# Scatter-adds of a graph diffusion that take turns over three accumulator tables in place of two

## The reference

```
h    = h @ W0.T + b0
deg  = segment_sum(ones, row) over row = [src, loops], col = [dst, loops]
dis  = 1 / sqrt(deg)
agg  = segment_sum(dis[row] * dis[col] * h[col], row)
x    = x + h + 0.05 * (agg - h) + 1.5 * relu(h)
```

## Time and profile before

| | us |
|---|---|
| median of 3 runs | 8765.82 |
| lowest and highest run | 8748.99, 8783.12 |
| span of the profiled execution | 7386.2 |
| what lies between the median and the span | 1379.6 |
| busy in the span: TensorE | 4675.6 (63%) |
| VectorE | 4503.1 (61%) |
| GpSimd | 3795.4 (51%) |
| ScalarE | 1623.3 (22%) |
| HBM read, written | 608.19 MB, 417.84 MB |

### The profile page before, as it was taken

One profiled execution on the slowest core, in us unless ns is written; L12 is line 12 of the kernel. 1 busy time (PEld: TensorE's weight loads), 2 busy tenths in 40 slices (PEclk: granted clock), 3 DMA queues, 4 the chain that ended last, 5 costly groups with the idle time before them and its releaser, 6 DMA issues. The chain is left out here.

```text
span 7386.2 us, 101314 instructions
## 1 busy us (share of the span) xinstructions
PE 4675.6 (63%) x31722; PEld 4192.0 (57%) x31722; DVE 4503.1 (61%) x5720; ACT 1623.3 (22%) x2242; POOL 3795.4 (51%) x3348
## 2 busy tenths in 40 slices
PE   4665335760188785555555866666668774784797
PEld 2354334650177785555555866666568774674675
DVE  6998443222577786666667842232398894683457
ACT  0143112330143343222222421111134340000001
POOL 0198565563277403777771047777600006766766
PEclk9866668995599998766767987777789996997899
DMA  2298666656722374332333753334357883122009
GB/s 75 48 276 259 140 147 140 138 108 201 252 73 73 101 245 154 83 79 79 81 78 101 249 164 109 109 109 112 100 186 250 304 307 112 49 59 91 14 12 278
DMA packets 837873, 1024.59 MB, mean 139 GB/s; under 512 B 589119, under 2 KB 601812, under 8 KB 836380
## 3 DMA queue, kind: packets, MB, share of 16 engines
q1 hardware_dynamic: 534716, 742.63, 31.5%
q0 software_dynamic: 144256, 90.12, 8.3%
q10 hardware_dynamic: 158560, 187.31, 7.6%
HBM read 608.19 MB, written 417.84 MB: 139 GB/s over the span
## 5 line engine op out<-in xcount | busy, mean ns | idle before, releaser
L839 POOL DMA_INDIRECT gc_msgs<-t,src_rows x784 | 754.4, 962 | 1098.1 <-POOLq L146 804.2
L893 POOL DMA_INDIRECT acc<-de_sums,de_put x392 | 608.5, 1552 | 410.9 <-DMA acc<-de_sums,de_put 263.5
L1913 PEld LDWEIGHTS gc_ring<-gc_msgs,gc_hot 128*128 128x128 f32 x4736 | 628.4, 210 | 305.9 <-issue 298.1
L1913 PE MATMUL gc_ring<-gc_msgs,gc_hot 128*128 x4736 | 654.9, 297 | 230.4 <-SPq L1872 229.3
L839 POOL DMA_INDIRECT at2s_ends<-h,src_rows x392 | 369.9, 944 | 533.6 <-POOLq L146 414.4
L839 POOL DMA_INDIRECT at1s_ends<-x,src_rows x392 | 389.2, 993 | 490.5 <-POOLq L146 371.3
L1027 PE MATMUL de_ring<-de_win,de_pick 128*128 x2368 | 343.2, 305 | 272.7 <-DMA de_win<-t 272.7
L1027 PEld LDWEIGHTS de_ring<-de_win,de_pick 128*128 128x128 f32 x2368 | 322.9, 217 | 295.0 <-issue 289.1
L839 POOL DMA_INDIRECT at1s_ends<-x,dst_rows x392 | 419.0, 1069 | 119.5 <-issue 119.5
L839 POOL DMA_INDIRECT re_rows<-x,src_rows x392 | 406.5, 1037 | 125.1 <-issue 124.8
L1393 PE MATMUL re_psR<-w_rel,re_own 128*128 128x128 f32 x3136 | 398.6, 293 | 73.6 <-DVE re_own L1330 73.3
(11 more groups left out here) (471 smaller groups left out, 11359.4 us busy)
## 6 DMA issues: line engine op xcount, KB each, us to landing
rew_win<-x SPq DMA_DIRECT2D x74, 544.0 KB, 4.0
at1w_win<-g SPq DMA_DIRECT2D x74, 544.0 KB, 4.0
at2w_win<-g SPq DMA_DIRECT2D x74, 544.0 KB, 4.0
de_near<-same SPq DMA_DIRECT2D x74, 512.0 KB, 5.1
de_win<-t SPq DMA_DIRECT2D x74, 512.0 KB, 4.6
x<-rew_win SPq DMA_DIRECT2D x74, 512.0 KB, 2.9
h<-at1w_win SPq DMA_DIRECT2D x74, 512.0 KB, 2.9
h<-at2w_win SPq DMA_DIRECT2D x74, 512.0 KB, 2.9
```

The lines of the kernel that those rows point to most:

```text
L839: nc.gpsimd.indirect_dma_start(buf[:, t * width:(t + 1) * width], None, table, bass.IndirectOffsetOnAxis(ap=rows[:, t:t + 1], axis=0)).the ...
L893: nc.gpsimd.indirect_dma_start(g.acc0[j % 2], bass.IndirectOffsetOnAxis(ap=put[:, j:j + 1], axis=0), sums[:, j * D:(j + 1) * D], None, com ...
L1913: done = nc.tensor.matmul(ring[:, bass.ds(to[n], SLOT)], hot[k][:, n, :], each_group(msgs[:, bass.ds(of[n], MID)], SLOT // MID), start=Fal ...
```

## The change

Tile `j` of the edge stage now goes to table `acc0[j % 3]` and waits until tile `j - 3` has landed. The third table is filled with zeros in the out-degree stage by 49 stores on SyncE's queue, gets a spare-row store in setup like the others, and in the close is loaded as a third operand (`more`) and added by one more VectorE operation a chunk.

```diff
+TURNS = 3
@@ build
-        g.acc0 = [node_table(f"acc0{k}", D) for k in range(2)]
+        g.acc0 = [node_table(f"acc0{k}", D) for k in range(TURNS)]
@@ setup
-                sp.wait_ge(attrs, 32 + 11 * 16)
+                sp.wait_ge(attrs, 32 + (9 + TURNS) * 16)
@@ out_degrees
+            @block.sync
+            def _(sp):
+                def clear(b):
+                    sp.dma_start(chunk_of(g.acc0[2], b.number), g.zeros[:, 0:J * D]).then_inc(zeroed, 16)
+                pipeline(sp, clear)
+                sp.wait_ge(zeroed, 16 * STEPS)
@@ diffusion_edges
-        added = [r.sem(f"added{k}") for k in range(2)]
+        added = [r.sem(f"added{k}") for k in range(TURNS)]
-                        if j >= 2:
-                            held(pool, added[j % 2], 16 * (j // 2), g.passed)
-                        nc.gpsimd.indirect_dma_start(g.acc0[j % 2], bass.IndirectOffsetOnAxis(ap=put[:, j:j + 1], axis=0),
-                                                     sums[:, j * D:(j + 1) * D], None, compute_op=ALU.add).then_inc(added[j % 2], 16)
-                for k in range(2):
-                    pool.wait_ge(added[k], 16 * (T // 2))
+                        if j >= TURNS:
+                            held(pool, added[j % TURNS], 16 * (j // TURNS), g.passed)
+                        nc.gpsimd.indirect_dma_start(g.acc0[j % TURNS], bass.IndirectOffsetOnAxis(ap=put[:, j:j + 1], axis=0),
+                                                     sums[:, j * D:(j + 1) * D], None, compute_op=ALU.add).then_inc(added[j % TURNS], 16)
+                for k in range(TURNS):
+                    pool.wait_ge(added[k], 16 * len(range(k, T, TURNS)))
@@ diffusion_close
-        base, acc = ([r.sb(f"{n}{k}", [P, W]) for k in range(SLOTS)] for n in ("base", "acc"))
+        base, acc, more = ([r.sb(f"{n}{k}", [P, W]) for k in range(SLOTS)] for n in ("base", "acc", "more"))
+                    sp.dma_start(more[b.slot][:, :], chunk_of(g.acc0[2], b.number)).then_inc(x_in[b.slot], 16)
-                    dve.wait_ge(x_in[s], 32 * b.nth)
+                    dve.wait_ge(x_in[s], 48 * b.nth)
                     link(nc.vector.tensor_tensor(base[s][:, :], base[s][:, :], acc[s][:, :], ALU.add))
+                    link(nc.vector.tensor_tensor(base[s][:, :], base[s][:, :], more[s][:, :], ALU.add))
```

More of the change, by code:

```diff
@@ L129 @@
 DMA_SIGNALS = {"loaded", "weights", "attrs", "zeroed", "o_stored", "x_in", "stored", "got", "ea_in", "seam_got", "seam_put", "last_in", "last_out", "path_put", "path_in", "line_put", "src_in", "same_put", "same_in", "win_in", "acc_in", "done_out", "base_in", "types_in",
-               ("de", "added0"), ("de", "added1"), ("dd", "cleared")}
+               ("de", "added0"), ("de", "added1"), ("de", "added2"), ("dd", "cleared")}
 class Room:
@@ L648, in out_degrees @@
         link_s = r.sem("link")
+        zeroed = r.sem("zeroed")
         with nc.Block() as block:
+            @block.sync
[4 more added lines that the diff above has]
+                sp.wait_ge(zeroed, 16 * STEPS)
             @block.gpsimd
```

## The result

Eleven runs of the changed kernel have a median of 8707.02 us (8678.69 to 8735.83), eleven of the kernel before 8772.87 us (8722.69 to 8795.15): 66 us faster by the medians. I had forecast 15 us faster, and 8707 lies under my range of 8722 to 8806.

What follows compares the result with a forecast made beforehand. No engine bounds the whole kernel, a row of stages; GpSimd's scatters end the edge stage, and DMA transfer fills the close. Scatters -84, close +69, fill and setup 0 sum to -15 us: 8765.8 to 8751 us, range 8722 to 8806.

Steps and rivals of the forecast that it cites:

- The scatters: Edge stage after tile 176: 30 of 113.6 us removable waits stay, last start 1655 us, gain 84 us (37 to 92).
- The door at tile 176: Edge stage, 1197.96 us: GpSimd had caught up with the copied sums, so only waits in the 216 scatters after it count.
- the free step: Edge stage, a scatter step that waits for nothing: 1.546 us of work and 0.44 between instructions, 1.99 us.
- The waits that stay: Edge stage after 1198 us: waits for a landing under 40 us in all, none above 1.3.
- Rival A: Edge stage: landings grow with a third transfer in flight, gain only 0 to 37 us, 8798 to 8835 us; chance 0.14.
- Rival D: Edge stage: the 78 waits aren't the table's turn, gain 0, the close still paid, 8835 us; chance 0.05.
- The sums' pace: Edge stage: denser scatters don't slow the 74 blocks, 0 us (-3 to +8), last block still near 1631.
- SyncE's late issue: Edge stage before 1198 us: window waits, 265.4 us in 23, come from SyncE first waiting for compares and their stores.
- The close: Final stage: the third load's transfer doesn't hide, 66 us plus 3 for the rest, 69 us (61 to 76).
- Rival B: Close: bound by its four slots' round trip, so the third load adds only 34 us, 8716 us; chance 0.07.
- Fill and setup: Out-degree stage and setup: the zero fill of 63 to 73 us and the extra pad are hidden, cost 0.
- The part outside the span: The runs' median lies 1379.6 us above the profiled span; nothing in the profile shows it, so left unchanged.

Runs made afterwards that it cites:

- lead3: The changed kernel (three tables) with SyncE's loads and the compares one block further ahead in the edge stage: 8676.44 us, ratio 0.9841 to the kernel before.
- add_only: The kernel before with the close's addition made twice, no third load or table: 8831.45 us, ratio 1.0016 to the kernel before.
- lead2: The kernel before, two tables, with SyncE's loads and the compares one block further ahead in the edge stage: 8778.13 us, ratio 0.9996.

## Why the prediction was wrong, by its own steps

**The scatters: right in mechanism, a little small.** The door at tile 176 held: waits before it were worth nothing and were turned into 99 us at the sums (75.1 and 24.0). The last scatter starts at 1647.81; I had 1655, and 1646.5 as the earliest. Of the 113.6 us that could go, more went than the 83.6 I took: the last batch of eight starts at 1634.85, 1.0 us behind the last copy of sums, so the gain is all that the sums allow. The term that was mis-sized is the free step. I read 1.99 us off steps part of which were still held by the two tables' turn; it is 1.85, so that the scatters had more to gain than I counted. The waits that stay were mis-sized the other way: the longest for a landing was 1.9 us against my 1.3, and all such waits 51.8 us against my 40. Rival A fell: it asked for a step above 2.40 us, and the step is 2.08. How long a scatter takes to land with three tables isn't known, as the view gives no landing time for them. Rival D fell with it. The Trainium skill's fit (DMA: Bandwidth & Descriptors, "Anatomy of one DMA"), by which a scatter of 32 KB lands in an estimated 2.1 us and two tables would never wait, fell too: landings took 3.0 us at the least, and with a third table 96 us of waits for them went. The turns are worth 91 us by the first profile, 98 by the mean of all.

**The sums' pace: right.** 1633.3 us for the last block after 1631.09, the same 23 window waits. That it was the limit is shown from both sides: four tables don't end sooner, a quicker pace with three tables ends 92 us sooner, and the same pace with two tables gives nothing. My reason for the pace before 1200 us, SyncE's late issue behind the compares, is shown by lead3 in kind and not in size: it is worth 3.8 us of the 20.3 us of a block, and what remains is VectorE's work.

**The close: this step failed.** I wrote that the transfer "doesn't hide, because the stage is little else", and priced it at the stage's own 350 to 376 GB/s, with 61 us as the lower end. I took the 0.95 busy share of the DMA engines for a full pipe. It was not full: its slices swung between 232 and 422 GB/s, and each chunk waited for a slot that came free only when a store had landed. Measured: 35 us between the two profiles as read, 31 against the mean of four unchanged closes, 30 (18 to 41) by the clock. Rival B had the mechanism and the number, 34 us, from the same rows, and I gave it 0.07. The price of 69 us holds for a close that is full: 63 us for the fourth load, and 251 - 187 = 64 us for the third when the slots are eight in both. The addition isn't free either, 14 us (6 to 21) by the clock in the close with two loads (add_only), where I had counted 3. It isn't that loads are cheap but that the kernel before left 31 us unused there. The 358 GB/s of the Trainium skill (DMA: Bandwidth & Descriptors, Specifications), named beside the sum, is passed by the 417 to 421 GB/s of these stages; only one core ran here.

**Fill and setup: right.** The fill takes about 65 us (13 slices of 5.2) of a stage of 202 that kept its length. The pads end at 76.3 instead of 75.1 and the path's store is not later.

**The part outside the span: wrong, without effect.** I left 1379.6 us alone as lying outside. They were the mark of one unusual execution; none of it touches the edit's stages. It is the close's 34 us and the scatters' 7 to 14 that make 8751 into 8707.

In sum: -84 + 69 should have been about -98 + 31 to 35.

## What to carry to other kernels

Don't price an added transfer by the rate a stage has, but ask whether that rate is the ceiling: a rate that swings from slice to slice (232 to 422 GB/s here) under a busy share of 0.95 leaves room, and the next load costs only what goes beyond it. That the issuing queue waits for slots doesn't tell the two apart: it did so for 144 us in the close with room, and for 158 us in the full one of the changed kernel:

```profile
SPq L1086 <- ACTq L1114: 157.7, 45, 11.0
```

What tells them apart is more slots: they shorten the one (216 to 187 us) and leave the other (252 to 251). Before a wait is counted as worth its length, find the last moment at which its engine stood at another door; only what comes after it can be gained, and the other door is then the cap. A step is free only if its gap doesn't shrink when the wait is eased. Lengths of one stage from one profile each can differ by 10 us with the same code, as this close does. And of two limits in line, taking away the second alone shows nothing (lead2), after the first it is worth 80 us.

## What the runs showed that I had not expected

The same program has executions that differ by 1383 us in the profile (spans 7386.2 and 8769.3 us), though its first 1700 us agree within 11. The gap lies in gather stages and in the last layer's sums, where TensorE's waits without a releaser go from 298.1 to 813.9 us between these two profiles:

```profile
PEld gc_ring L1913 <- issue: 298.1, 141, 31.5
```

```profile
PEld gc_ring L1913 <- issue: 813.9, 425, 31.8
```

The matmuls of that stage are no slower (297 and 287 ns on the mean), so the added time is idle time. The mean granted clock over the span is 0.816 in the first and 0.767 in the second; whether that is a cause of the idle time or comes of it isn't known. None of the 72 timed runs of the kernel before lies under 8722 us. What makes the difference is open; no run here was made for it.
